# The 3x3 kernels' sums on TensorE, the statistics chain over more rounds, earlier loads, and output stores issued by ScalarE

## What is computed

```python
# layer 0, on the group norm of x (32 groups)
f = relu(einsum('oc,nchw->nohw', Wc, x) + bc)                     # 512 -> 128 channels
gk1 = relu(mean(x, (2, 3)) @ Wc.T + bc)
g_kern = gk1[:, :, None] * Wkk + bkk                              # (N, 128, 9)
xm = x.reshape(N, C, 3, 16, 3, 16).max(axis=(3, 5))
sk = relu(einsum('oc,nckl->nokl', Wc, xm) + bc)
dynW = relu(einsum('oj,ncjkl->nockl', Wck, stack([g_kern, sk], 2)) + bck)   # 3x3 kernels, per image
y = conv3x3(f, dynW) + b_ad
x1 = x + einsum('oc,nchw->nohw', Wf, y) + bf                      # 128 -> 512 channels
# layer 1, on the group norm of x1: 3x3 convolution in 32 groups of 16 channels
out = x1 + conv3x3_grouped(group_norm(x1), kernels)
```

## Time and profile before

| | |
|---|---|
| median of 3 runs | 4095.43 us (4094.3 to 4110.99) |
| the profiled execution's own time | 4124.97 us |
| its span | 4123.2 us |
| busy: PE, DVE, ACT, POOL | 3635.4 (88%), 2730.7 (66%), 2124.2 (52%), 946.1 us (23%) |
| DMA | 667.00 MB, 162 GB/s over the span |

### The profile page before, as it was taken

One profiled execution on the slowest core, in us unless ns is written; L12 is line 12 of the kernel. 1 busy time (PEld: TensorE's weight loads), 2 busy tenths in 40 slices (PEclk: granted clock), 3 DMA queues, 4 the chain that ended last, 5 costly groups with the idle time before them and its releaser, 6 DMA issues.

```text
span 4123.2 us, 60550 instructions
## 1 busy us (share of the span) xinstructions
PE 3635.4 (88%) x18432; PEld 2837.3 (69%) x18432; DVE 2730.7 (66%) x6196; ACT 2124.2 (52%) x3495; POOL 946.1 (23%) x1036
## 2 busy tenths in 40 slices
PE   3788998889998889998888998889988899988896
PEld 2666777667776667776666777667766677766674
DVE  6766676666676666767676766666766667676642
ACT  3355555555554555455555455555545544555554
POOL 2022222222122222122222122222222221222223
PEclk9899999999999999999999999999999999999998
DMA  4465655665655756656756656657557566566555
GB/s 102 130 172 161 183 162 154 175 167 159 186 148 146 201 150 176 169 155 157 200 150 174 170 148 164 169 158 189 155 139 197 151 175 172 145 163 181 152 139 128
DMA packets 318393, 667.00 MB, mean 162 GB/s; under 512 B 59314, under 2 KB 289076, under 8 KB 289460
## 3 DMA queue, kind: packets, MB, share of 16 engines
q1 hardware_dynamic: 318132, 663.46, 60.2%
HBM read 355.12 MB, written 308.28 MB: 161 GB/s over the span
## 4 chain that ended last, share of the span: by engine, by line
issue 65%; POOL 20%; PE 8%; DVE 3%; DMA 2%; ACT 1%; POOLq 1%; SPq 0%; DVEq 0%; ACTq 0%
POOL hl L398 19%; PE pb L869 1%; PE pb L871 1%; PE pb L870 1%; DMA big<-x_rows 1%; POOLq L397 1%; PE pac L869 1%; PE pd L869 1%; PE pd L871 1%; PE pd L870 1%; DVE big L779 1%; PE pac L871 0%; PE pac L870 0%; DMA out<-big 0%; DVE bst L583 0%
## 5 line engine op out<-in xcount | busy, mean ns | idle before, releaser
L398 POOL TENSOR_TENSOR hl<-un,hl 128x384 f16<-128x384 f32 x1024 | 918.7, 897 | 3098.7 <-ACT hl L423 3098.2
L419 ACT ACTIVATE un<-big,b_t,s_t 128x384 f32<-128x384 f32 x1024 | 711.1, 694 | 387.3 <-DMA big<-x_rows 379.5
L423 ACT ACTIVATE hl<-un 128x384 f16<-128x384 f32 x1024 | 539.0, 526 | 360.8 <-PE pb L871 267.7
L869 PE MATMUL pd<-hl,k_h 128*96 128x384 f16 x1536 | 540.2, 352 | 172.6 <-POOL hl L398 172.6
L869 PE MATMUL pb<-fh,dynh 128*128 128x480 f32 (+1 forms) x1440 | 551.2, 383 | 31.3 <-DVE xs L755 31.2
L779 DVE SCALAR_TENSOR_TENSOR big<-pb,kout,big 96x768 f32<-96x768 f32 x256 | 259.1, 1012 | 474.2 <-PE pb L871 474.2
L779 DVE SCALAR_TENSOR_TENSOR big<-pd,kout,big 96x768 f32<-96x768 f32 x256 | 258.8, 1011 | 460.3 <-PE pd L871 460.3
L871 PE MATMUL pb<-fh,dynl 128*128 128x480 f32 (+1 forms) x1440 | 545.9, 379 | 0.0
L870 PE MATMUL pb<-fl,dynh 128*128 128x480 f32 (+1 forms) x1440 | 544.7, 378 | 0.0
L871 PE MATMUL pd<-hl,k_l 128*96 128x384 f16 x1536 | 538.0, 350 | 0.0
L870 PE MATMUL pd<-hl,k_h 128*96 128x384 f16 x1536 | 537.6, 350 | 0.0
(11 more groups left out here) (111 smaller groups left out, 5604.1 us busy)
## 6 DMA issues: line engine op xcount, KB each, us to landing
big<-x SPq DMA_DIRECT2D x128, 1152.0 KB, 19.4
x_rows<-x1b SPq DMA_DIRECT2D x128, 1152.0 KB, 5.7
big<-x_rows SPq DMA_DIRECT2D x128, 1152.0 KB, 10.6
out<-big SPq DMA_DIRECT2D x128, 1152.0 KB, 5.7
big<-x_rows SPq DMA_DIRECT2D x256, 192.0 KB, 11.5
x_rows<-mrow SPq DMA_DIRECT2D x64, 96.0 KB, 8.9
big<-kt SPq DMA_DIRECT2D x4, 288.0 KB, 11.4
big<-kt SPq DMA_DIRECT2D x2, 192.0 KB, 10.7
```

Of the source, the lines that this page charges most:

```text
L398: pool.tensor_tensor(hl[:, g % HL_RING, 1, :, 1:W + 1], un[:, g % U_RING], hl[:, g % HL_RING, 0, :, 1:W + 1], ALU.subtract).then_inc(hl_lo, 1)
L419: act.activation(un[:, g % U_RING], t_slot(g // GQ)[:, g % GQ], ACT.Identity, bias=b_t[:, g:g + 1], scale=s_t[:, g:g + 1]).then_inc(u_done, 1)
L423: act.activation(hl[:, g % HL_RING, 0, :, 1:W + 1], un[:, g % U_RING], ACT.Copy).then_inc(hl_hi, 1)
L869: pe.matmul(acc, high_w, high_x, start=start, stop=False)
```

## The change

- **Sums.** `kernel_inputs` now makes 18 rows (9 of the maxima, 9 copies of the mean) by 128 columns with the bias as a fifth matmul. ScalarE makes `gates` of them (`gate_rows`, after group 30: relu, then an affine pass by row). TensorE forms all nine sums as three fp32 matmuls of 19 rows by 384 columns (`dyn_kernels`, after round 14) into the three banks of `pac`. The VectorE operations of `dyn_inputs`, `dyn_maxima` and `dyn_global` go. `dyn_high` and `dyn_low` read `pac`, so `dyn_low` moves to the end of the step, and TensorE waits for `dyn_done` ahead of A instead of ahead of B.
- **Statistics chain.** `prep_means` at round 6, `group_mean` after 7, `prep_variances` at 8, `group_variance` after 9, `x1_means` at 8, `x1_group_means` at 10, its matmul after 9; the latter now also waits for the next image's `root_first`, which moves from group 22 to group 24.
- **First `xs`.** The high parts are made after groups 26, 28 and 30, the low parts in rounds 13, 14 and 15.
- **SyncE.** x loads 1, 2 and 3 go before, between and behind the loads of chunks 0 and 1, and no longer wait for `x1_done`; the load of chunk 2 goes ahead of `write_x1(n, 2)`.
- **Stores.** ScalarE issues them: chunk 0 after group 13, 1 after group 21, 2 after group 29, 3 in the next A behind `x_high` 6. In the drain likewise.

```diff
-ROOT_AFTER = 22
+ROOT_AFTER = 24
+GATES_AFTER = 30
+STORE_AFTER = {13: 0, 21: 1, 29: 2}
+LAST_STORE_AT = 6
...
@@ sync step
+                if more:
+                    load_x(n + 1, 1 - odd, 1)
                 if d:
...
-                    for c in range(2):
-                        load_t(n - 1, c)
+                    load_t(n - 1, 0)
                 if more:
-                    for c in STATS_IN_B:
-                        load_x(n + 1, 1 - odd, c)
-                for c in range(2):
-                    write_x1(n, c)
-                    if more and c in STATS_LATE:
-
-                        load_x(n + 1, 1 - odd, c)
+                    load_x(n + 1, 1 - odd, 2)
                 if d:
-                    store(n - 1, 0)
-                write_x1(n, 2)
+                    load_t(n - 1, 1)
+                if more:
+                    load_x(n + 1, 1 - odd, 3)
+                write_x1(n, 0)
+                if more:
+                    load_x(n + 1, 1 - odd, 0)
+                write_x1(n, 1)
                 if d:
                     load_t(n - 1, 2)
+                write_x1(n, 2)
                 write_x1(n, 3)
                 if d:
-                    store(n - 1, 1)
                     load_t(n - 1, 3)
                 write_means(n)
-                if d:
-                    store(n - 1, 2)
-                    store(n - 1, 3)
...
@@ scalar
+            def store(n, c):
+                dst, made = out[n, c], n * PAIRS + (c + 1) * PER_CHUNK
+                act.wait_ge(out_done, made)
+                act.dma_start(dst, t_slot(c)[0:M6].rearrange("p j b w -> p (j b w)")).then_inc(stored[c], 16)
...
                     if d:
                         d_groups(n - 1, [g])
+                        if g in STORE_AFTER:
+                            store(n - 1, STORE_AFTER[g])
...
+                    if g == GATES_AFTER and more:
+                        gate_rows(n + 1)
+                    for i in X_HIGH_AFTER.get(g, ()) if more else ():
+                        x_high(n + 1, 1 - odd, i)
...
@@ vector
-            def x1_group_means(n):
-
+            def x1_group_means(n, more):
+
+                if more:
+                    vec.wait_ge(sd_done, n + 2)
                 vec.wait_ge(stat_mm2, 2 * n + 1)
...
@@ tensor
+            def dyn_kernels(n):
+
+                pe.wait_ge(gates_done, n + 1)
+                for i in range(C_BANKS):
+                    ins = pe.matmul(dyn_acc[:, i, :], gates[0:GATES + 1, :], wrow[0:GATES + 1, i * 3 * CM:(i + 1) * 3 * CM],
+                                    start=True, stop=True)
+                ins.then_inc(dyn_mm, 1)
...
             def step(n, odd, d=True, more=True):
                 pe.wait_ge(wc_done, n + 1)
-                reached(pe, x1_done, n * CUNITS)
+                pe.wait_ge(dyn_done, n + 1)
                 for t in range(NT):
                     a_tile(n, t)
-                pe.wait_ge(dyn_done, n + 1)
```

More of the change, by code:

```diff
@@ L67 @@
 MAXIMA_AT = {5: 0}
[L68 to L71, removed]
+PREP_MEANS_AT = 6
+PREP_VARIANCES_AT = 8
+X1_SUMS_AT = 8
+X1_MEANS_AT = 10
 PREP_SCALED_AT = 11
+GROUP_MEAN_AFTER = 7
+GROUP_VARIANCE_AFTER = 9
+KERNEL_INPUTS_AFTER = 12
+KERNELS_AFTER = 14
+X_HIGH_AFTER = {26: (0, 1), 28: (2, 3), 30: (4,)}
+X_LOW_AT = {13: (0, 1), 14: (2, 3), 15: (4,)}
+GATES = 2 * TAPS
 def x_slot(c, odd):
@@ L125, in build @@
         wfl = sb("wfl", [P, C], F32R)
-        rows = sb("rows", [P, 3, CM])
+        gates = sb("gates", [P, CM])
+        wrow = sb("dyn_rows", [P, TAPS * CM])
+        bcr = sb("bcr", [P, CM])
         ind = sb("ind", [P, GC, GQ])
@@ L154, in build @@
         b_t = sb("b_t", [P, G])
-        pac = [bank(f"pac{i}") for i in range(C_BANKS)]
+        pac = ctx.enter_context(nc.psum_tensor("pac", [P, C_BANKS, 512], F32))
         pb = ctx.enter_context(nc.psum_tensor("pb", [P, 2, 512], F32))
@@ L366, in _ @@
             images(sp, step)
-            for c in range(2):
+            for c in range(Q):
                 load_t(N - 1, c)
[L369 to L373, removed]
             for c in range(Q):
@@ L465, in root_second, with gate_rows @@
                                scale=XSCALE ** -2).then_inc(sd2_done, 1)
+            def gate_rows(n):
+                act.wait_ge(stat_mm, 3 * n + 3)
+                act.activation(gates[0:GATES, :], ps[0:GATES, 128:128 + CM], ACT.Relu).then_inc(gates_relu, 1)
+                act.wait_ge(gates_relu, n + 1)
+                act.activation(gates[0:GATES, :], gates[0:GATES, :], ACT.Identity, bias=kks[0:GATES, 1:2],
+                               scale=kks[0:GATES, 0:1]).then_inc(gates_done, 1)
             def dyn_high(n):
[L468 to L469 removed]
+                act.wait_ge(dyn_mm, n + 1)
+                act.activation(dynh_banks, dyn_acc, ACT.Relu).then_inc(dyn_hi, 1)
             def kernels(i):
@@ L485, in step @@
                             x_high(n, odd, i)
+                        if i == LAST_STORE_AT and (not isinstance(n, int) or n >= 2):
+                            store(n - 2, Q - 1)
                     if t:
@@ L515, in _ @@
             root_second(N - 1)
-            d_groups(N - 1, range(G))
+            store(N - 2, Q - 1)
+            for g in range(G):
+                d_groups(N - 1, [g])
+                if g in STORE_AFTER:
+                    store(N - 1, STORE_AFTER[g])
+            store(N - 1, Q - 1)
         @block.vector
@@ L788, in step @@
                         f_low(n, t - 1)
-                    if t == DYN_LOW_AT:
-                        dyn_low(n)
                 f_low(n, NT - 1)
@@ L822, in step @@
                             prep_variances(n + 1)
+                    if r == X1_SUMS_AT:
+                        x1_means(n)
+                    if r == X1_MEANS_AT:
+                        x1_group_means(n, more)
+                    if more:
                         if r == PREP_SCALED_AT:
@@ L827, in step @@
                             prep_scaled(n + 1, 2)
-                        if r == PREP_SCALED_AT + 2:
-                            dyn_inputs(n + 1)
-                            for part in DYN_HALVES:
-                                dyn_maxima(n + 1, part)
-                        if r == PREP_SCALED_AT + 3:
-                            for part in DYN_HALVES:
-                                dyn_global(n + 1, part)
+                        for i in X_LOW_AT.get(r, ()):
+                            x_low(n + 1, 1 - odd, i)
                 if more:
-                    for i in range(AHEAD):
-                        x_low(n + 1, 1 - odd, i)
+                    dyn_low(n + 1)
             memsets()
@@ L849, in _ @@
                 prep_scaled(0, i)
-            dyn_inputs(0)
-            for part in DYN_HALVES:
-                dyn_maxima(0, part)
-            for part in DYN_HALVES:
-                dyn_global(0, part)
             for i in range(AHEAD):
                 x_low(0, 0, i)
+            dyn_low(0)
             images(vec, step)
@@ L995 @@
     from concourse.bass_utils import run_bass_kernel_spmd
+    kks = np.zeros((GATES, 2), np.float32)
+    kks[0:TAPS, 0] = 1.0
+    kks[TAPS:, 0] = np.asarray(L0_conv_Wkk)
+    kks[TAPS:, 1] = np.asarray(L0_conv_bkk)
+    wck = np.asarray(L0_conv_Wck)
+    wrow = np.zeros((GATES + 1, TAPS, CM), np.float32)
+    for k in range(TAPS):
+        wrow[k, k] = wck[:, 1]
+        wrow[TAPS + k, k] = wck[:, 0]
+    wrow[GATES] = np.asarray(L0_conv_bck)
     laid_out = {
```

122 lines of the change are left out of this document (46 added, 76 removed).

## The result

The change takes 4452.2 us, median of 4 runs (4451.11 to 4453.28), against 4101.14 us before, median of 4 runs next to it: a ratio of 1.0855, with a 95% interval of 1.0834 to 1.0876. The forecast was 4540 us with a range of 4430 to 4650; the time lies in the range, 88 us under the forecast, and on the side that was given 0.94.

A forecast was written before the change was run, and what follows sets the result against it. It took serial store-to-load waits for late chunks as the bound: 15.5 us an image, taken as 14.5, 435 us over thirty images, 449 with last step and drain, on 4124.97, corrected for a profiled run 0.7% high: 4540 us, range 4430 to 4650.

The forecast's parts named there:

- The mechanism: Last stage: store 1 behind group 21 needs chunk 2, so two store-to-use ways run in series; chunk 3 11.9 us late.
- signs named for being right: ScalarE's DMA wait 750 to 850 us in two pieces over 10 us, chunk 3 17 to 18 us after store 1, period 138 to 141.
- The size of a leg: From a chunk's store to ScalarE's first use of the chunk reloaded into its slot: 6.0 plus 11.8, 17.8 us.
- X: Zero of the forecast's times: TensorE's end of group 9, for which ScalarE's copy of group 13 waits.
- The discount to the mean image: Loss per image lowered from 15.5 to 14.5 us, as part of the mean image's surplus is late chunks now covered.
- The base: The 449 us were added to the profiled 4124.97 us, 0.7% above the median 4095.43; that difference was to carry over.
- VectorE's queue of 8.2 us: Round 10: VectorE waits for the root behind group 24; means, an output and scaling delay kernel inputs 8.2 us after chunk 3.
- The sums: After round 14: three new fp32 matmuls on TensorE's path cost 1.9 us an image, with 0.5 us as lower bound.
- The edge and A: Image's edge: TensorE's wait becomes about 3.5 us for `dyn_low` (+0.3); the first 1x1 product gets 0.8 us shorter.
- The statistics chain: Before group 24: means and variances get a round more before TensorE, in time spent waiting for chunk 3; worth nothing.
- rivals** by quicker transfers: Shorter store-to-use ways: still slower, 4300 us (chance 0.08); faster, 4025 us (0.04); no change, 4110 us (0.02).
- the one by slower transfers: Stores and loads of two rings slow each other, 15 us a load; worse than the range, chance 0.06.

The follow-up runs named there:

- runs in halves: Every chunk store and load split into two of four groups with own semaphores: kernel before 3881.76 us; the change, stores back on SyncE, 3910.54 us.
- in a better order: The change with split stores and loads on SyncE, root behind group 24, x1's mean moved ahead of the variances: 3794.45 us.
- before in halves: The kernel before with every chunk store and load split into two of four groups each, with semaphores of their own: 3881.76 us.

## Why the prediction was right, and where it was not

- **The mechanism** was the one predicted. Both legs now stand in line with 9.15 us of groups between them (9.5 predicted), the DMA wait is 773.4 us (750 to 850), in two pieces an image. Of the 351 us, the stores alone bring 280, all but the stores brings 27, and moving store 1 alone takes 321 away. Three of the signs named for being right came out smaller than said: the first piece of the wait is 9.66 us and not over 10, chunk 3 is used 16.6 us after store 1 and not 17 to 18, and the period is 135.5 us and not 138 to 141. None of the signs of being wrong came.
- **The size of a leg** is the first term that was too large: 17.8 us, measured 16.4 and 16.6. The store is 0.35 us quicker to its load. The load is used 10.7 and 10.9 us after its issue instead of 11.8. With the 0.4 us by which ScalarE sends store 0 sooner than assumed, and 0.35 us less for groups 16 to 21, chunk 3 comes at X+42.3 instead of X+45.7 (X+33.8 before): 3.4 us an image. The forecast kept the old leg on the ground that the drain, with empty rings, showed 17.7 too. In the drain of the change it is shorter as well (store at 4324.03, use at 4340.78: 16.75 us). Most of the difference is the choice of the image. Over images 6 to 29, store 1 to load is 5.96 us in the mean before and 5.68 in the change, and load to first use 11.3 (10.7 to 12.1) and 11.1 us (10.5 to 11.7): a leg of 17.3 us against 16.8. Before's image has a leg 0.5 us above its mean, the change's one 0.2 below. Why the remaining 0.5 us are gone stays open.
- **The discount to the mean image.** The step from 15.5 to 14.5 us an image was a guess at how much of before's surplus is late chunks. The image read grew by 12.1 us (123.6 to 135.7), which is the 15.5 less the 3.4 just named, the small terms as a whole being right; the mean image lost 10.2. The discount should have been 2, since before's mean image was 1.7 to 2.1 us longer than the one read (125.3 over the loop, 125.7 over its second half, against 123.6), and the change's is not (135.5 against 135.7). The two errors explain the 128 us by which the loop was forecast too dear (435 against 307), while the ends were forecast too cheap (14 against 21.5 us).
- **The base, and luck.** The sum was 4124.97 + 449 = 4574 us, and 34 us were then taken off because the profiled execution of before was 0.7% above the median. That did not carry over: the four executions of the change lie within 2.2 us, the profiled one at 4453.28. Against it the sum was 121 us too high; the 34 us, taken off for a reason that did not hold, hid part of this and left the 88.
- **VectorE's queue of 8.2 us was the wrong reason with the right number.** The kernel inputs do start 8.2 us after chunk 3 is used, and VectorE does wait for the root (316.9 us in all). Yet with the root back, the 8.2 us remain. The queue itself was done 6.0 us after chunk 3 (2179.40): the means took 1.0 us instead of 1.9, the scaling 2.4 instead of 3.7. The 8.2 us are the way to TensorE and its two groups at half clock after the long idle; that the two sums agree is luck. The step failed by following one queue into a place where another, TensorE's own, ends last. The forecast counted the idle time of a wait, but not what the clock takes afterwards, which is 2.8 us at this one place (5.93 against 3.16).
- **The sums**: 2.20 us against 1.9, six records as in the upper bound, wholly on the path. A record costs 0.37 us there, near the 0.32 that the forecast took as its upper bound.
- **The edge and A**: 3.09 us of wait for `dyn_low` and 15.2 us for A with its first bias matmul. The forecast had 3.5 us with the bias matmul and 15.3 us behind it, 18.8 in all; measured are 18.3. The wait did change its owner from `xs` to `dynl`.
- **The statistics chain** was put at nothing, and with the root's place the change's time does not move (4456.58 against 4452.2 us); what the earlier rounds give was not run by itself. The runs in halves show what the order is worth once no chunk is late. Root and mean in the order of the change cost 84 to 116 us, a good part of it by the clock; in a better order the sums, the chain and the earlier loads together win 87 us over before in halves (3881.76 to 3794.45).
- **The rivals** by quicker transfers fell: a leg of 16.5 us is far from the 10 us at which the sign would turn. (At 9 us the prediction's own terms give a gain of 2.1 us an image, not 2.3.) So did the one by slower transfers, 15 us a load. The prediction's estimate of 10.3 us for a leg uses a fit that the page of the Trainium skill (DMA: Bandwidth & Descriptors, Anatomy of one DMA) gives for DMAs issued by GpSimd, while these are issued by SyncE and ScalarE, so it was no test of that fit.

## What to carry to other kernels

When a transfer's issue moves into the queue of an engine that consumes the buffer, ask whether it now stands behind work that needs the other buffer: two legs that lay beside each other become a chain, and the place counts, not the queue. Where a slot is used again, halves with semaphores of their own shorten the way from store to use, here for 5.4%. And a wait of TensorE costs more than its idle time: look at the granted clock behind it, and at short VectorE operations that run beside GpSimd on its way.

## What the hardware showed unexpectedly

- ScalarE's store was issued at 2131.32, while the pass ahead of it in program order still ran (2131.11 to 2131.64): the issue waited for `out_done` and its turn, not for the end of that pass.
- An operation of 128 x 4 elements on VectorE took 770 ns in the mean beside a GpSimd subtraction and 169 ns without; in the image shown it started 0.11 us after GpSimd's and ended 0.03 us after it. The Trainium skill (SBUF — State Buffer, Who interferes with whom) has GpSimd share one pair of ports with VectorE, and for the forms of VectorE's operations that use this pair, whichever engine issues first holds it for its whole instruction; the trace agrees for this operation.
- TensorE's granted clock fell to half behind an idle of 1.67 us in 22 of 31 images and behind one of 1.01 us in none of 30, at the same place of the program. It also fell within or right behind twelve fp32 records of 19 rows with no idle at all, in 18 of 31 images, and in the steady loop not with six. Why is not settled.
- Store 1 landed 2.0 us later (7.7 us to the next load's issue against 5.7, means of 24 images) with its early place than with its late one, at 301 GB/s in one such stretch (2127.78 to 2135.30) against 209 GB/s (2156.83 to 2162.48). The load behind it took 11.1 us to its first use in both.
